# The steady pass of a six-stage transformer pipeline, laid out in another order on four engines

## The reference, cut to what matters

```
x  = L0_attn_x                        # (32, 256, 128)
xn = layernorm(x)
x  = x + attn0(xn) + ffn0(xn)         # attn0: 16 heads of 8, windows of 128 keys, plus attention to 64
                                      # pooled tokens, mixed by a sigmoid gate; ffn0: ternary weights
xn = layernorm(x)
qkv = xn @ W_qkv + b_qkv              # attn1: 16 heads of 8
time, space = expmap0(q or k)         # cosh and sinh of a Minkowski norm
dist   = arccosh(max(time_q*time_k - space_q.space_k, 1 + 1e-7))
attn   = softmax(-dist**2 / sqrt(8), causal) * (sigmoid(xn @ w_sur + b_sur) > threshold)
h = silu(xn @ w1) * (xn @ w2)         # ffn1: 128 -> 512
h = gelu(h @ h1); h = gelu(h @ h2)    # 512 -> 512, twice
x = x + (attn @ v) @ W_out + b_out + h @ w3
```

## Time and profile before

| | us |
|---|---|
| median of 3 runs | 1998.73 |
| lowest and highest | 1990.13, 2000.18 |
| the profiled execution, its own time | 1992.87 |
| its span, first to last instruction | 1990.1 |
| busy: TensorE | 1738.8 (87%) |
| busy: VectorE | 1621.5 (81%) |
| busy: ScalarE | 1537.8 (77%) |
| busy: GpSimd | 1012.7 (51%) |

### The profile page before, as it was taken

The page is one execution under the profiler, slowest core; times in us unless marked ns, Lnnn a source line. Parts: engine busy times, 40 slices in busy tenths (PEclk is TensorE's granted clock), DMA queues, the critical chain, the costliest instruction groups (busy, mean ns, idle before and its releaser), DMA issues.

```text
span 1990.1 us, 53659 instructions
## 1 busy us (share of the span) xinstructions
PE 1738.8 (87%) x18914; PEld 1346.4 (68%) x18914; DVE 1621.5 (81%) x3565; ACT 1537.8 (77%) x2117; POOL 1012.7 (51%) x1176
## 2 busy tenths in 40 slices
PE   4568898999899899989989998998999899899888
PEld 2346676677677667767766776776777676677667
DVE  7778888888888888888888888888888888888785
ACT  8327787878788787878878778877878787877687
POOL 5336554456654445665544565544556554455432
PEclk9779999999999999999999999999999999999899
DMA  7333133323223332322333232233223133323110
GB/s 210 113 88 85 51 92 89 84 59 85 79 58 88 88 84 61 84 80 58 88 88 85 60 83 66 69 88 90 69 69 90 56 80 88 84 54 89 46 46 7
DMA packets 302218, 155.77 MB, mean 78 GB/s; under 512 B 14644, under 2 KB 298196, under 8 KB 302036
## 3 DMA queue, kind: packets, MB, share of 16 engines
q1 hardware_dynamic: 302164, 155.06, 28.9%
HBM read 83.18 MB, written 71.30 MB: 78 GB/s over the span
## 4 chain that ended last, share of the span: by engine, by line
PE 48%; DVE 28%; issue 10%; ACT 10%; SPq 1%; POOL 1%; DVEq 1%; DMA 0%; ACTq 0%; POOLq 0%
PE pu L2322 16%; PE pav L2164 3%; DVE nmax L786 3%; PE pav L2138 3%; PE pav L2162 2%; PE pm L2304 2%; PE pu L2123 2%; DVE zc L979 2%; PE pm L2191 2%; DVE hid L1000 2%; DVE hid L993 2%; ACT L1835 2%; DVE poly L941 1%; DVE u_qk L919 1%; DVE v_both L1018 1%
## 5 line engine op out<-in xcount | busy, mean ns | idle before, releaser
L1424 POOL TENSOR_TENSOR zs<-zc,zs 128x1024 f32<-128x1024 f32 x160 | 376.3, 2361 | 142.0 <-ACT zc L1713 142.0
L2322 PE MATMUL pu<-hid,h1t 128*128 128x256 f32 x1024 | 257.9, 396 | 1.2 <-DVE nmax L786 1.2
L2322 PE MATMUL pu<-hid,h2t 128*128 128x256 f32 x1024 | 240.4, 383 | 4.1 <-DVE hid L1000 4.1
L1402 POOL TENSOR_TENSOR emb<-xn,w_sur 128x256 f32<-128x256 f32 x32 | 23.3, 727 | 381.6 <-PE pm L2191 381.6
L2322 PEld LDWEIGHTS pu<-hid,h1t 128*128 128x128 f32 x1024 | 188.4, 193 | 39.6 <-issue 15.3
L2322 PEld LDWEIGHTS pu<-hid,h2t 128*128 128x128 f32 x1024 | 188.4, 192 | 27.0 <-issue 4.7
L1712 ACT ACTIVATE zs<-zc,mhalf 128x1024 f32<-128x1024 f32 x160 | 182.3, 1139 | 0.6 <-DVE zc L979 0.2
L1713 ACT ACTIVATE zc<-zc,phalf 128x1024 f32<-128x1024 f32 x160 | 181.7, 1136 | 0.0
L773 DVE TENSOR_REDUCE zmin<-pu 128x8 f32<-128x1024 f32 (+2 forms) x123 | 150.0, 1220 | 30.0 <-DVE hid L1000 17.0
L1733 ACT ACTIVATE zs<-zs 128x1024 f32<-128x1024 f32 x160 | 166.9, 1047 | 0.0
L979 DVE TENSOR_SCALAR zc<-pu 128x1024 f32<-128x1024 f32 x123 | 149.1, 1212 | 0.0
(11 more groups left out here) (351 smaller groups left out, 4918.2 us busy)
## 6 DMA issues: line engine op xcount, KB each, us to landing
scr<-parts SPq DMA_DIRECT2D x256, 192.0 KB, 2.1
q_st<-scr SPq DMA_DIRECT2D x128, 256.0 KB, 3.8
scr<-parts SPq DMA_DIRECT2D x128, 128.0 KB, 2.1
k_st<-scr SPq DMA_DIRECT2D x64, 256.0 KB
k_st<-scr SPq DMA_DIRECT2D x32, 512.0 KB, 4.9
x<-in_L_attn_x SPq DMA_DIRECT2D x32, 128.0 KB, 2.9
out<-xold SPq DMA_DIRECT2D x32, 128.0 KB, 1.8
q_st<-m_t SPq DMA_DIRECT2D x128, 4.0 KB
```

Source lines behind the costliest of these rows:

```text
L1424: G.tensor_tensor(zs[:, c], zc[:, c], zs[:, c], ALU.add).then_inc(sum_done.sem, 1)
L2322: last = PE.matmul(u.ap[:, c * T:(c + 1) * T], w[:, k, c * P:(c + 1) * P], src[:, k, :], start=(k == 0), stop=(k == HC - 1))
```

## The change

The blocks are the same, with one exception, and their order in `iteration` is new on four engines; SyncE's stays. The homes of the results in the five PSUM buffers are new too. The exception is `single_values`: its two copies leave VectorE and become two activations with `Copy` on ScalarE, in the steady pass and in three of the closing passes.

```diff
-        U0_USES = uses("early", ["z0", "z2", "z3"]) + uses(M, ["exp1", "exp2"]) + uses(L, ["min2"]) + uses(M, ["avT0"]) + uses(L, ["min3", "min4"]) + uses(E, ["sub3"]) + uses(F, ["max2", "max4"]) + uses(M, ["f1_2"]) + uses("late", ["z7"])
+        U0_USES = uses("early", ["z0", "z2", "z3"]) + uses(M, ["exp5", "exp0", "exp4"]) + uses(L, ["min2", "min3"]) + uses(E, ["sub2", "sub4"]) + uses(F, ["max2", "max3"]) + uses(M, ["f1_0"]) + uses("late", ["z7"])
...
-            def single_values(run, l):
-
-                dve.wait_ge(v1_ready.sem, v1_ready.at(l))
...
-                V.tensor_copy(v_both[0:QW, :, :, 0:HD], v_mid[0:QW, :, 0:D].rearrange("p k (s e d) -> p k s e d", e=2, d=HD)[:, :, :, 0, :])
-                V.tensor_copy(v_both[QW:P, :, :, 16:16 + HD], v_mid[QW:P, :, D:D + QW].rearrange("p k (s d) -> p k s d", d=HD)).then_inc(vboth_ready.sem, 1)
...
                 if e:
                     spiked_norm(avuse(run, "avT1"), y1, link[E])
-                if l:
-                    single_values(run, l)
...
+            def single_values(run, l):
+
+                act.wait_ge(v1_ready.sem, v1_ready.at(l))
...
+                for e, cols in enumerate((v_mid[0:QW, :, 0:D].rearrange("p k (s e d) -> p k s e d", e=2, d=HD)[:, :, :, 0, :], v_mid[QW:P, :, D:D + QW].rearrange("p k (s d) -> p k s d", d=HD))):
+                    last = S.activation(v_both[e * QW:(e + 1) * QW, :, :, 16 * e:16 * e + HD], cols, ACT.Copy)
+                last.then_inc(vboth_ready.sem, 1)
...
                     root(run, l, 3)
...
+                    single_values(run, l)
                     root(run, l, 4)
```

More of the change, by code:

```diff
@@ L343, in build @@
         uses = lambda stage, names: [(stage, n) for n in names]
-        U0_USES = uses("early", ["z0", "z2", "z3"]) + uses(M, ["exp1", "exp2"]) + uses(L, ["min2"]) + uses(M, ["avT0"]) + uses(L, ["min3", "min4"]) + uses(E, ["sub3"]) + uses(F, ["max2", "max4"]) + uses(M, ["f1_2"]) + uses("late", ["z7"])
[L345 to L348, removed]
+        U0_USES = uses("early", ["z0", "z2", "z3"]) + uses(M, ["exp5", "exp0", "exp4"]) + uses(L, ["min2", "min3"]) + uses(E, ["sub2", "sub4"]) + uses(F, ["max2", "max3"]) + uses(M, ["f1_0"]) + uses("late", ["z7"])
+        U1_USES = uses("early", ["z1"]) + uses(M, ["exp1"]) + uses(L, ["min1"]) + uses(E, ["f3"]) + uses(L, ["min4"]) + uses(E, ["sub3"]) + uses(F, ["max1"]) + uses(L, ["f2"]) + uses(M, ["f1_2"]) + uses("late", ["z4", "z5"])
+        AV_USES = uses(L, ["min0"]) + uses(M, ["exp2", "exp3", "av0", "avT0"]) + uses(E, ["sub0", "sub1"]) + uses(F, ["max0"]) + uses(E, ["av1", "avT1"]) + uses(F, ["max4", "max5"]) + uses("late", ["z6"])
+        MISC_USES = [uses(F, ["xT", "qk"]) + uses("weights", ["extremes"]) + uses(E, ["mT1"]) + uses(F, ["v"]) + uses(M, ["qkv1a"]) + uses(F, ["rqkv"]) + uses(E, ["yT", "y1"]),
+                     uses(O, ["yffn"]) + uses(M, ["lexp", "lo", "rem", "mixT", "y0", "x1T", "qkv1b", "embT"]) + uses(F, ["lmax", "mT"])]
         CLOSING_USES = {
@@ L1039, in iteration @@
                 if l:
-                    minima(run, 1)
+                    clamp_cosh(run, 0)
                 if m:
@@ L1090, in iteration @@
                     window_maxima(run, 0)
+                if a:
+                    dve.wait_ge(x_in.sem, x_in.at(a))
+                    moments(st, mv, ve, x, LN_EPS, var0, link[N])
+                if l:
+                    clamp_minima(run, link[L])
+                if f:
                     window_maxima(run, 1)
+                    window_maxima(run, 2)
+                    latent_projections(run, f)
                 if m:
@@ L1216, in closing @@
                 spiked_norm(avuse(r0, "avT1"), y1, k0[E])
-                single_values(r0, r0.last)
                 gate_values(r0, r0.middle, "f1_2", (2, 3), k0[M])
@@ L1257, in closing @@
                 spiked_norm(avuse(r1, "avT1"), y1, k1[E])
-                single_values(r1, r1.last)
                 attention_out(r1, r1.end)
@@ L1280, in closing @@
                 spiked_norm(avuse(r2, "avT1"), y1, k2[E])
-                single_values(r2, r2.last)
                 clamp_cosh(r2, 4)
@@ L1919, in closing @@
                 copied(avuse(r0, "av1"), o_t[:], avuse(r0, "av1").ap.rearrange("p (v t) -> p v t", v=2)[:, :, 0:T])
+                single_values(r0, r0.last)
                 root(r0, r0.last, 3)
@@ L2430, in iteration @@
                     first_scores(unit(run, "max1"), 1)
+                    window_scores(unit(run, "max2"), 2)
                 if m:
```

192 lines of the change are left out of this document (93 added, 99 removed).

## The result

The changed kernel takes 1911.24 us, the median of four runs (1909.78 to 1914.36), beside 1996.28 for the kernel before in four runs (1990.13 to 2000.18). The ratio is 0.958, with a 95% interval of 0.955 to 0.961. I had forecast 1955, half of that gain. Run again on another occasion, the changed kernel took 1909.72.

A forecast was written before the change was run, and what follows sets the result against it. Waits between engines bound the kernel; after the change a loop over `min0` of 54.0 + 3.2 = 57.2 us against 58.4 saves 36 over 30 passes, plus some 4 in closing passes: median 1955, range 1892 to 2040.

The forecast's parts named there:

- The copies: Moving both `single_values` copies from VectorE to ScalarE: saves 0.4 us of work and a stall of up to 1.4 a pass.
- `spikes`: Moved behind `attended` on VectorE, its second one-column instruction is caught by `split0`'s last piece: some 1.0 us of waiting a pass.
- The transfers: SyncE's write and read back between the end of `split1` and `min0`: 11.2 us of the loop.
- The catch beside the norm chain: Seven SBUF-to-SBUF VectorE instructions from `clamp_minima` to `split1` stall beside GpSimd's norm work: 3.2 us a pass, bounds 0 and 5.9.
- The loop over `min0`: From `min0` through VectorE's work, `split1` and its transfers back to `min0`: 57.2 us, setting the length of a pass.
- The catch is light: Rival, chance 0.27: the five small VectorE encounters with GpSimd mostly miss, TensorE sets the pass at 55.6 us, total 1905.
- the 1.0 at `mixT`: TensorE's wait at `mixT` from the caught `spikes` on VectorE: 1.0 us a pass.
- the four waits that I had put at 2.0: TensorE's remaining waits in the new order, at `min1`, layer 1's projections, `av1` and `f2`: 2.0 us a pass, bounds 1 to 4.
- The further 0.7 at `f2`: In the light-catch case, TensorE's `f2` waits for `max1`, which stands behind L968 on VectorE: 0.7 us a pass.
- The slower rival: Chance 0.24: `normed` begins ahead of L969, the last of `split1` falls behind the first `sum_cosh`; loop 59.9 us, total 2034.

## Why the prediction was wrong

The direction was right and the size was not: 81 us in 28 passes, where I had said 36 in 30. The 1911 us lie inside my range of 1892 to 2040, but that range reached down so far only for a rival. Point by point.

**The copies: right in the old order, and nearly in size.** I had put their stall and work at up to 1.4 a pass. It measured 1.14. That they cost nothing on ScalarE was wrong in the new order, where they cost 0.5; I had given 0.6 as the price without cover, and named 10.4 us of idle time as the cover, without asking whether that idle time lay in the stretch where they stand. It does not: from `root(0)` to `shift_part` ScalarE has hardly a pause.

**`spikes`: right.** Forecast was 1.0 us, with L961 caught by the last piece of `split0`. Measured: 1.01 in place of 0.23, and both end together (1188.85 and 1188.82). TensorE waits 0.95 at `mixT`.

**The transfers: right.** 11.2 forecast, 11.1 measured.

**The catch beside the norm chain: the step that failed.** The text says: "L968 meets `power` (0.65 lost)" and "The other five each meet a piece of 0.3 to 0.8, at 0.5 on average: 2.5. Together 3.2." Measured: 0.13. I took a stall for as long as what is left of GpSimd's operation by its row. That holds for a sum of 128x1024, from which I had the rule. It does not for a power of two columns, which costs nothing, nor for a norm of 0.79, which costs 0.15 at most. The rows that showed a catch, to the earlier trace rows, stood beside sums, beside the last piece of `split0`, and, for L737, beside the addition `xres` of 0.72 us. All of these have two inputs of 256 columns or more, and I applied them to operations of much the same duration that have not. To look up which operation stood beside each row would have shown it. With 0.13 in its place (11.7 - 3.2 + 0.13), the stretch from `max0` to the end of `split1` is 8.6, and measured it is 8.4 (1209.00 to 1217.43).

**The loop over `min0`: it exists, it does not bind.** Its terms in the changed kernel are 4.5 from `min0` to the end of `clamp_cosh(0)` (1173.95 to 1178.49; forecast 3.5, and the second half of `yffn` now stands behind `exp5` and its wait), 30.5 on to `max0` (30.8), 8.4 (11.7) and 11.1 (11.2). That is 54.5, 0.9 below the pass. The first test that the prediction named for itself, "If TensorE does not wait at `min0`, the loop is not the bound, and I am wrong towards the faster side", is what happened.

**The rival that came in.** "The catch is light" gave 55.6 and 1905; measured were 55.45 and 1911. Of its terms, the 1.0 at `mixT` is in the trace (0.95), and the four waits that I had put at 2.0 measure 1.5: `min1` 0.2, layer 1's projections 0.5, `av1` 0.4, `f2` 0.5. The further 0.7 at `f2`, for L968 caught by `power`, is not there, since L968 is not caught. In its place stand waits that are in no sum of mine: 0.9 at `exp5`, 0.3 for `hid` and 0.2 for `xn`. The sum of the waits comes to 3.9 for 3.7, out of other terms, and the wait at `exp5` is among those that hold the pass. I had walked through TensorE's waits for PSUM homes and through the large transfers, and not through the small rows that SyncE writes behind `shift_part`. The agreement to 6 us is luck in good part.

**The slower rival** named a real price and the wrong way to it. With `split1` 3.0 us later, behind `spiked_norm`, it fell behind the first sum, and 207 us were lost. But `normed` ahead of L969 could not have brought that about: a norm cost none of the five forms tried more than 0.15, and in the changed kernel L750 ends at 1161.97, 1.4 us ahead of the first sum at 1163.33.

What stays open is how the 49 us of the new order divide. They are not the clock for the most part: at full clock the pass is 57.17 with the copies moved alone and 55.45 in the changed kernel, 1.72 less, of the 1.76 between the means (57.25 and 55.49). Of the 1.72, TensorE's idle time gives 1.3 (5.2 to 3.9) and its busy time 0.4 (51.93 to 51.52). Some stalls are gone: L737 took 0.69 once in every pass and never goes over 0.171 now, as the prediction had counted, and L806 no longer meets a sum, which by itself had cost nothing. Nothing took the rest apart, since the orders of four engines and the PSUM homes changed together.

## What to carry to other kernels

The price of a meeting of VectorE and GpSimd is not the length of GpSimd's row. Ask what the GpSimd operation reads. Here a power of two columns cost nothing, a norm or product of one input of 128 columns and a copy of 256 at most 0.23 us, while one with two inputs of 256 columns or more was sat out to its end, and sums of 128x1024 one after the other cost nearly their whole length to each instruction of VectorE that followed. So what matters is whether a block of VectorE lies ahead of the first large operation of GpSimd or behind it; in one kernel here 0.08 us decided that, in every pass alike. And before an idle share is named as the cover of added work, look at the stretch where it goes in, and follow every transfer that a waiting engine needs, the smallest too: here four transfers of 4 KB stood on the path of every pass, and not the large ones beside them. And measure two parts of a change apart where you can: here the part that helped in the old order did harm in the new one.

## What the runs showed of the hardware that I had not expected

- A GpSimd power on 128x2 lasts 0.69 us and lengthens no VectorE instruction, of five forms, by more than 0.03 us. A norm of 128x128 lasts 0.79 and lengthens one by at most 0.15. A sum of 128x1024 lasts 2.34 and lengthens each by up to 2.2. An addition of two inputs of 128x256 lasts only 0.72 and lengthened a 128x2 instruction by 0.52, to its own end.
- The loss can fall on GpSimd: the power took up to 1.24 us beside subtractions of 128x512, the copy of `values1` 0.80 for 0.40 beside `split1`.
- Meetings that look like chance repeat exactly once the order leaves no slack: where the copies of `single_values` began just ahead of a sum (the second by 0.08 us), the first of them kept 208 to 210 ns in all 29 passes, and the second 224 or 225.
